# Node groups in order of their size, and the node work of a group put among the second graph sum's quads

## What is computed

```python
x = x + _L0_gnn_ref(_layernorm(x, axis=-1), edge_index, edge_weight, ...)
x = x + _L0_ffn_ref(_layernorm(x, axis=-1)[None], ...)[0]
x = x + _L1_gnn_ref(_layernorm(x, axis=-1), src, dst, ...)
x = x + _L1_ffn_ref(_layernorm(x, axis=-1)[None], ...)[0]
```

```python
h = jax.nn.relu(gcn_conv(x, src, dst, ew, W1, b1))       # 256 -> 64 channels
z = jax.nn.relu(gcn_conv(h, src, dst, ew, W2, b2))       # 64 -> 32 channels
d = jax.nn.relu(z @ Wd1 + bd1)                           # 32 -> 64
x_hat = jax.nn.sigmoid(d @ Wd2 + bd2)                    # 64 -> 256
```

## Time and profile before

| | us |
|---|---|
| median of three runs | 8922.13 |
| the runs | 8907.27, 8923.36, 8922.13 |
| span of the profiled execution | 8907.5 |
| first gather to last addition, second sum | 2811.09 to 4894.77 |
| first gather of attention | 5860.51 |

### The profile page before, as it was taken

How to read it: one execution, slowest core, us unless ns; L and a number is a source line. 1 busy time by engine, 2 the same in 40 slices (tenths; PEclk the granted TensorE clock), 3 DMA queues, 4 the chain that set the end, 5 groups by cost and what they waited for, 6 DMA issues and landing times. The chain is left out here.

```text
span 8907.5 us, 139784 instructions
## 1 busy us (share of the span) xinstructions
PE 4910.0 (55%) x21452; PEld 3757.5 (42%) x21453; DVE 4675.9 (52%) x13784; ACT 2359.3 (26%) x5395; POOL 5054.9 (57%) x5289
## 2 busy tenths in 40 slices
PE   4744444444434444444443799956666666664079
PEld 3643333333333333333333455544444444443056
DVE  6854444444433344333333533357777777777821
ACT  1223333333341000000000533333333333333511
POOL 0037777777762777777777000057777777774241
PEclk6555555555555555555555899977777777776589
DMA  3122222222232000000001000146666666664420
GB/s 72 34 57 78 79 80 78 78 79 80 78 92 70 13 13 13 13 13 13 13 13 13 12 19 21 47 152 186 186 186 189 188 183 187 185 190 142 135 78 20
DMA packets 504367, 752.32 MB, mean 84 GB/s; under 512 B 159558, under 2 KB 288894, under 8 KB 504188
## 3 DMA queue, kind: packets, MB, share of 16 engines
q0 software_dynamic: 198928, 349.25, 16.5%
q1 hardware_dynamic: 244460, 285.91, 10.4%
q10 hardware_dynamic: 60800, 115.36, 3.7%
HBM read 566.05 MB, written 184.06 MB: 84 GB/s over the span
## 5 line engine op out<-in xcount | busy, mean ns | idle before, releaser
L724 POOL DMA_INDIRECT conv_rows<-table,conv_idx x3328 | 3149.0, 946 | 1182.0 <-issue 1013.0
L778 PE MATMUL conv_pm<-conv_rows,conv_sel 128*128 x7040 | 1704.6, 415 | 2531.9 <-SPq L741 2459.2
L778 PEld LDWEIGHTS conv_pm<-conv_rows,conv_sel 128*128 128x128 f32 x7040 | 1567.1, 327 | 2669.5 <-issue 2669.5
L1630 POOL DMA_INDIRECT att_rows<-ft_rows,att_idx x1760 | 1680.2, 955 | 1558.7 <-ACT att_idx L1647 971.5
L767 DVE TENSOR_TENSOR acc<-acc,conv_pm 128x64 f32 (+1 forms) x3520 | 719.2, 204 | 1982.9 <-PE conv_pm L778 1195.2
L1802 PE MATMUL att_pm<-att_rows,att_sel 128*128 128x264 f32 x3520 | 1285.4, 521 | 102.0 <-DVE sums L1943 90.4
L751 DVE TENSOR_SCALAR conv_sel<-iota,edges,edge_w 128x128 f32<-128x128 f32 x3528 | 1009.8, 356 | 520.8 <-issue 494.9
L1802 PEld LDWEIGHTS att_pm<-att_rows,att_sel 128*128 128x128 f32 x3520 | 855.0, 259 | 404.4 <-DVE sums L1943 153.4
L704 ACT ACTIVATE conv_idx<-sources 128x8 int32 x416 | 86.7, 208 | 3330.6 <-SPq L741 2967.0
L1943 DVE TENSOR_TENSOR sums<-sums,att_pm 128x264 f32 x1760 | 749.5, 426 | 340.4 <-PE att_pm L1802 288.1
L1912 DVE TENSOR_TENSOR att_rows<-att_rows,att_pw 128x1056 f32<-128x1056 f32 x440 | 539.3, 1245 | 38.1 <-issue 21.6
(11 more groups left out here) (362 smaller groups left out, 5884.7 us busy)
## 6 DMA issues: line engine op xcount, KB each, us to landing
selections<-conv_hot ACTq DMA_DIRECT2D x220, 512.0 KB
att_sel<-selections SPq DMA_DIRECT2D x440, 256.0 KB
att_bc<-places SPq DMA_DIRECT2D x110, 512.0 KB
conv_rows<-table,conv_idx POOLq DMA_INDIRECT x3328, 2.4
att_rows<-ft_rows,att_idx POOLq DMA_INDIRECT x1760
ft_rows<-proj_ft SPq DMA_DIRECT2D x25, 544.0 KB, 3.0
x_normal<-elu_xr SPq DMA_DIRECT2D x25, 514.0 KB
x_spilled<-x_rows SPq DMA_DIRECT2D x25, 512.0 KB, 2.9
```

What stands on the lines that cost most here:

```text
L724: pool.indirect_dma_start(out=rows[:, k, :], out_offset=None, in_=table, in_offset=bass.IndirectOffsetOnAxis(ap=idx[:, k % AHEAD:k % AHEAD ...
L778: ins = nc.tensor.matmul(pm[q][:, i, :], sel[:, q * QUAD + i, :], rows[:, ds(slots[i], 1), :].rearrange("p a c -> p (a c)"), start=True, s ...
L1630: pool.indirect_dma_start(out=rows[:, at % SLOTS, :], out_offset=None, in_=K.ftd, in_offset=bass.IndirectOffsetOnAxis(ap=idx[:, at:at + 1] ...
```

## The change

**Schedule.** The 25 groups are ranked by the number of their tiles, and the steps are laid out in that order, the group with the fewest first. For this the count of tiles of each group comes from a matmul, ranks and first steps from comparisons and two small matmuls, and every step's number is shifted by its group's offset before the comparisons that find its tile. A tile that two groups share is gathered for both, so a graph sum has 1688 gathers instead of 1664 (the number is a constant, and so is the place by which each quad's gathers are in: `arrived_by`). The sources are gathered with a second set of 14 gathers and kept as integers in the order of the gathers, so that a gather takes its index from them with no copy by ScalarE.

**Graph sums.** GpSimd's and SyncE's parts are written out without loops. TensorE loads one register word for a quad instead of two. In the first sum ScalarE's one-hot matrices no longer wait for the gathers.

**First table.** SyncE issues a copy of x inside DRAM (12.8 MB) behind the first four groups' loads and ahead of the others.

**One phase in place of four.** Second sum, decoder, mixture and projection become `nodes`. After the first 18 quads, the first group's sums are complete. Then 25 segments follow, each with the node work of one group (read from and written back to the copy in DRAM) among the 17 or 18 quads of the next group; the last has no quads. The node work has single buffers, and the products of a quad have two PSUM buffers instead of four, since PSUM also holds the mixture's. The weights are 31 transfers on SyncE ahead of its counting. VectorE makes the selections of each quad as before.

```diff
...
+LEAST = GW - 1
+GATHERS = -(-(STEPS - LEAST * (GROUPS - 1)) // SECT) * SECT
...
+            tt(less[:, :], less[:, :], tied[:, :], ALU.add).then_inc(less_ready, 1)
+            dve.wait_ge(ranked, 1)
+            own.then(dve.tensor_copy(ranks[:, :], tp[1][0:G, 0:2]))
...
+            sp.dma_start(K.xd[0:N, :], x).then_inc(spilled, 16)
...
+def arrived_by(step):
+
+
+    return step - LEAST * (step * GROUPS // STEPS) + 1
...
+    counted = [arrived_by(q * QUAD + QUAD - 1) for q in range(QUADS)]
+    for j in range(0, GATHERS, SECT):
+        free = j + SECT - SLOTS + LEAST * GROUPS
+        if free > 0:
+            pool.wait_ge(mm_done, free)
+        if j >= LANES:
+            pool.wait_ge(arrived, 1 + next(q for q in range(QUADS) if counted[q] >= j + SECT - LANES))
+        pool.sem_inc(taken, 1)
+        for k in range(j, j + SECT):
+            pool.indirect_dma_start(out=rows[:, k % SLOTS, :], out_offset=None, in_=table,
+                                    in_offset=bass.IndirectOffsetOnAxis(ap=K.srct[:, k:k + 1], axis=0)
+                                    ).then_inc(gathered[k % LANES], 16)
+
...
-    return slots, pe.value_load(K.landed[0:1, ds(quad, 1)], min_val=LANES + 1, max_val=LANES + TB * P)
...
+    FIRST = [-(-QUADS * (j + 1) // GROUPS) for j in range(GROUPS + 1)]
+    LENGTHS = [FIRST[j + 1] - FIRST[j] for j in range(PER_TURN)]
...
+        pm = [ph.ps(f"pm{i}", [P, QUAD, C]) for i in range(2)]
         px = ph.ps("px", [P, 2, GW * P])
-        ring = [ph.ps(f"ring{i}", [P, GW * P]) for i in range(BANKS)]
-        pg = ph.ps("pg", [P, GW * P])
...
+            with eng.Fori(0, TURNS - 1) as t:
+                for j in range(PER_TURN):
+                    segment(t * PER_TURN + j, t * TURN_QUADS + FIRST[j], FIRST[j], t, LENGTHS[j])
...
+            def products(q, at_, lap, n):
+
+                for i in range(n):
+                    bank, slot = (at_ + i) % 2, (at_ + i) % RING
+                    slots = quad_slots(pe, K, q + i)
+                    pe.wait_ge(arrived, q + i + 1)
+                    pe.wait_ge(sel_ready, q + i + 1)
+                    if not isinstance(q, int) or q + i > 1:
+                        pe.wait_ge(added, q * QUAD + i * QUAD)
+                    for k in range(QUAD):
+                        ins = mm(pm[bank][:, k, :], sel[:, slot * QUAD + k, :],
+                                 rows[:, ds(slots[k], 1), :].rearrange("p a c -> p (a c)"), start=True, stop=True)
+                    ins.then_inc(mm_done, QUAD)
...
+                sums(2)
+                latent(n)
+                sums(1)
+                widen(n)
+                sums(1)
+                decoded(n)
+                sums(3)
+                rows_turned(n, 0)
+                sums(1)
+                logits(n)
+                for m in range(3):
+                    first(n, m)
+                sums(1)
+                for m in range(3, L1):
+                    first(n, m)
+                sums(1)
+                second(n)
+                gates_turned(n)
+                sums(1)
+                gates_spread(n)
+                experts(n)
+                sums(1)
+                mixed(n)
+                sums(3)
+                rows_turned(n, 1)
+                sums(1)
+                projected(n)
+                sums(more)
+            turns(pe, segment)
 
...
+                act.wait_ge(o_done, n + 1)
+                act.activation(sg[:, :, :], po, ACT.Sigmoid).then_inc(sig_done, 1)
+                rooting(n, 0)
+                normal_rows(n, 0)
...
+            def add(q, at_, n):
+
+                for i in range(n):
+                    s = q * QUAD + i * QUAD
+                    ws = quad_windows(dve, K, q + i)
+                    select((at_ + i + 1) % RING, s + QUAD)
+                    dve.wait_ge(mm_done, s + QUAD)
+                    for k in range(QUAD):
+                        to = K.acc2[:, ds(ws[k], 1), :].rearrange("p a c -> p (a c)")
+                        dve.wait_ge(added, s + (k + QUAD))
+                        tt(to, to, pm[(at_ + i) % 2][:, k, :], ALU.add).then_inc(added, 1)
...
+                scale(n, q)
+                sums(4)
+                dve.wait_ge(sig_done, n + 1)
+                dve.wait_ge(x_loaded, n * 16 + 16)
+                own.then(tt(xg[:, :, :], xg[:, :, :], sg[:, :, :], ALU.add))
+                statistics(n, 0)
+                sums(1)
+                inverses(n, 0)
+                sums(2)
+                columns(n, 0)
+                sums(1)
+                gates(n)
+                sums(3)
+                gated_experts(n)
+                sums(1)
+                dve.wait_ge(out_done, n + 1)
+                own.then(tt(xg[:, :, :], xg[:, :, :], po, ALU.add))
+                statistics(n, 1)
+                sums(1)
+                inverses(n, 1)
+                sums(2)
+                columns(n, 1)
+                sums(more)
+                assert own.k == PER, own.k
+            turns(dve, segment)
 
 
...
-            graph_sum(nc, K, "conv2", K.t2, K.acc2, CH2, a["x"])
...
-            decode(nc, K, a["L0_gnn_b2"], a["L0_gnn_Wd1"], a["L0_gnn_bd1"], a["L0_gnn_Wd2"], a["L0_gnn_bd2"])
...
-            mixture(nc, K, a)
...
-            project(nc, K, a["L1_gnn_W"], a["L1_gnn_attn_l"], a["L1_gnn_attn_r"])
...
+            nodes(nc, K, a)
...
```

1001 lines of the change are left out of this document (455 added, 546 removed).

## The result

The changed kernel takes **8218.5 us** (median of four runs, 8216.9 to 8219.7) against 8914.7 before (four runs, 8904.2 to 8923.4): a ratio of 0.9218, with a 95% interval of 0.9205 to 0.9231. The forecast was 8553 with a range of 8210 to 8910. The direction was right, and so was the engine pair that sets the pace; the gain was 696 us where 369 were forecast, and the result lies 8 us above the lower end of the range.

The account below looks back on a forecast made before the run. VectorE, TensorE and GpSimd taking turns were to set 103 us a segment: phase -432, schedule +35, first sum +18, first table +10, together -369 us, span 8538, median 8553 us, range 8210 to 8910.

Parts of the forecast that it names:

- GpSimd's 84.4 us: New phase: GpSimd's time per segment, 67.5 gathers at 1.25 us each.
- The likeliest case: New phase: TensorE's clock at 0.75, segments of 103 us (94 to 112), kernel 8553 us; chance 0.60.
- the fast clock: Rival, new phase: clock near 1.00, GpSimd nearly the bound, segments of 88 us, kernel 8193 us; chance 0.17.
- VectorE's own 74.0 us: New phase: VectorE's work per segment, 57.0 us for 17.6 quads at 3.24 plus 17.0 of node work.
- The stalls: New phase: VectorE's waits for node-work pieces, 14, 29 or 44 us a segment at full, middle or half clock.
- forecast's own columns: New phase: each piece's stall listed at full clock, midway and half clock; mixed outputs, for example, 3.8, 6.5, 9.3 us.
- The cover: New phase: one quad of VectorE work, 3.24 us, hides that much of each TensorE piece; 3.2 is subtracted per stall.
- The half clock throughout: Rival, new phase: clock at 0.50, segments of 122 us, phase 49 us longer, kernel 9034 us; chance 0.12.
- slower gathers: Rival, new phase: VectorE's selections slow GpSimd, a group's gathers take 121 us, kernel about 9010 us; chance 0.06.
- The signs it named: New phase: GpSimd busy above 75%, TensorE above 70%, clock near 0.75, gathers 950 ns, VectorE's largest waits named.
- Schedule and first table: Before the first sum: schedule +35 us (25 to 50) for ranks and second gathers, copy of x +10 (0 to 60).
- First sum: First graph sum: 24 more gathers +30 us, ScalarE's one-hot tail gone -12, together +18.

Follow-up runs that it names:

- the half-gather run: Changed kernel with every other gather of the second sum left out after the first 128, using old rows: 8212.6 us, a segment 90.4 us.
- the doubled first layers: Changed kernel with each of the mixture's first-layer products made twice, to the same result: 8473.0 us, a segment 100.6 us.
- the filler: Changed kernel plus four useless TensorE products behind most quads of a segment, to raise the clock: 8230.3 us, ratio 0.9230; 0.9221 on the slow chip.
- the early exponential: Changed kernel with ScalarE taking the gates' second exponential after the first of the ring's results instead of the third: 8215.0 us, ratio 0.9218.
- the run above: Changed kernel with the copy of x in DRAM issued at the start of the first graph sum, not in the first table: 8226.2 us, ratio 0.9214.

## Why the forecast was right, and where it was off

**The engines that set the pace: right.** The forecast had VectorE and TensorE in turns above GpSimd's 84.4 us, and the half-gather run shows that.

**The time: inside the range, in part by luck.** The likeliest case had 8330 to 8770 for itself and 94 to 112 us for a segment; 8218.5 and 90.5 lie below both. The whole range holds the result only because its lower end was drawn down towards the fast clock, and the clock of that rival, near 1.00, didn't come.

**VectorE's own 74.0 us: nearly.** 90.5 less 18.3 of stalls are 72.2. A quad back to back takes 3.08 us in this code and not 3.24, which is 2.8 less for 17.6 quads. The node work is 1.0 more than 17.0, and as much is idle time ahead of the scaling (24.7 us in 22 segments), which the forecast hadn't. Nearly half of it, 11.7 us, is at the three places where the loop turns:

```profile
DVE nod_u L1357 <- issue: 24.7, 12, 4.1
```

**The stalls: 29 forecast, 18.3 measured.** The largest places are those forecast for four of seven: the second exponential 5.7 (4.7 forecast), the mixed outputs 3.7 (6.5), behind the projection 3.7 (5.3), the experts 1.5 (3.8). Two cost nothing: the second three first layers (6.1) and the second layer (1.6). The sigmoid costs 2.7 (0.7), and the logits' 1.0 wasn't forecast.

**The step that was off is the clock, taken as one value for all pieces.** The forecast put 0.75 on every piece. The mean over the segments is 0.70, even a little lower, but it isn't a mean that acts. In the segment shown the clock is at the full level from the end of the first layers' first eight rows through the mixed outputs, where TensorE has no gap and its time is on the path one for one (the doubled first layers), and mostly at the half level in the rest, where VectorE has the quads and TensorE waits for it. By the forecast's own columns, the five places from the second exponential to the mixed outputs at the full clock are 11.2 us (3.8 + 2.3 + 3.2 + 1.8 + 0.1), and 11.9 were measured there with the logits. Projection and decoder at the half clock are 9.4 (7.8 + 1.6), and 6.4 were measured; the projection lies across a rise. Together 20.6 for 18.3, where the one value gave 29. The sums fit, the single places don't: the second exponential is 5.7 for 2.3, the second three first layers 0 for 3.2. This is worked out from the traces. No run changed the clock and nothing else, since the filler's own time comes with it, so how much of the 12.5 us between 103 and 90.5 is the clock's isn't shown by a run. The earlier trace rows had both levels, but not which pieces of the new order would get which.

**The cover was a second error, of the other sign in places.** 3.2 us per piece holds roughly where TensorE has gaps. In the stretch without gaps the stalls are one sum, TensorE's time less VectorE's, which moves from place to place (the early exponential).

**The rivals.** The fast clock's 8193 lies closest to the result, but its reason isn't what happened: the granted clock is 0.70, not near 1.00. The half clock throughout didn't come, nor did slower gathers: 955 ns, 0.30 between two, with VectorE 51% busy, where the forecast expected over 70%. So no slowing by the port rule of the Trainium skill (SBUF — State Buffer, Who interferes with whom) is seen in this phase either; whether any of VectorE's instructions here takes that port, no run shows.

**The signs it named.** GpSimd's share is 71% and not above 75%, TensorE's 78% (above 70% as forecast), the gathers are at 955 ns, and VectorE's largest waits are for the second exponential, which comes behind first layers, and for the mixed outputs.

**ScalarE's table loads: right at nothing.** 88 loads in 22 segments at 1283 ns, half of them ahead of a square root, which are the ones shown (ScalarE's groups, 3000 to 5000 us):

```profile
L1243 ACT ACT_TABLE_LOAD x44 | 56.5, 1283 | 0.8
```

The last group has a square root with no quad beside it:

```profile
5101.45 0.18 DVE L1372 RECIPROCAL nod_rs<-nod_rs 128x4 f32<-128x4 f32 x1 [0.42 <-ACT nod_rs L1243]
```

VectorE was idle for 0.42 us between statistics and inverse, into which the root's 0.30 fits, but no load: the load was made while ScalarE waited for the statistics. The other three loads of a segment are early as well: ahead of the sigmoid, for instance, the load ends at 4116.98, and the sigmoid starts at 4120.42, when TensorE's output is there. The Trainium skill, ScalarE: Activation LUTs, What ACT_TABLE_LOAD costs, has about 2.66 us for a switch to a different set. The trace here has its 1.28 for the load, shows nothing of the drain, and has none of it on the path.

**Schedule and first table: +45 forecast, +23.8 measured.** The copy was 0 instead of 10, by the run above. The first statistics of the first table are at 157.11 instead of 132.55, +24.6, where the schedule was to cost 35: the ranks took 20 and not 25 us (comparisons start at 40.48 instead of 20.44), and the second gathers and row products 4.6 and not 10.

**First sum: +18 forecast, +19.9 measured.** **Attention: +8 us** with no change in its code; its first to last gather take from 2277 to 2295 us over these kernels, against 2270 before, the chip of the 12116 us left aside. Why it is longer in all of them stays open; the order of the steps is other than before, which no run tests.

**The offset.** The forecast added 14.6 us between span and median, as before's runs had it; the changed kernel's median is 2.8 above its span, which is 12 us of the distance from the forecast.

## What to carry to other kernels

Where work of one engine is woven into another's waiting, find the stretches in which one engine has no gap: there its time counts one for one and single waits can't be saved, only work of the other engine moved in; where it has gaps, each wait that is split away pays. Take the clock of TensorE by piece, not as a mean: with a mean of 0.70 the same 128x512 products took 6.59 us for eight rows at the start of their run and 1.88 for the next four. And when an engine is 93% of the pace, test with its work halved before calling it the bound, and compare segment by segment: a mean difference of 0.9 us was nearly all in the last four of 24.

## What was not expected of the hardware

One chip ran the kernel before in 12116 us instead of 8915. The kernel with the filler had gathers as long there as elsewhere (mean granted clock 0.62, and 0.67 on the other chip), but waits between instructions: 1105 us ahead of VectorE's additions in the first sum alone. Its ratio to before was 0.922 there, and 0.923 on the other chip. Why that chip is slower stays open.

And TensorE's granted clock rises and falls several times within 90 us, at nearly the same pieces each time. The first layers in the segment after the one shown, changed kernel:

```profile
4228.46 6.39 PE L1129 MATMUL nod_big<-nod_xt,nod_sw 128*128 128x512 f32 x8
4234.68 1.88 PE L1129 MATMUL nod_big<-nod_xt,nod_ew 128*128 128x512 f32 x4
```

6.39 and 1.88 us, where it was 6.59 and 1.88: long in the first four products (eight rows), short from the fifth on.
